# Shared experts of two batches behind the dense experts, the last shared product behind the expert loop, a vector-engine bias, down weights as 128 and 48 rows, and a new order of stages

## The reference

```python
x = x + attention(norm(x))      # q = x Wq + bq, (k, v) = x Wkv + bkv; per token: softmax over 16 heads of q.k, times v
x = x + dense_experts(norm(x))  # 2 experts, 1024 hidden; each token goes to the one with the larger gate
x = x + state_scan(norm(x))     # delta = softplus(...); h = dA * h + dBu along the 512 tokens, 8 states; y = h.C + x * D
x = x + experts64(norm(x))      # 64 experts, 176 hidden, 6 per token, + a shared expert of 352 hidden for all tokens
```

## Time and profile before

| | before |
|---|---|
| median of 3 runs | 772.27 us (769.51 to 773.78) |
| the profiled execution | 767.52 us, of which 765.4 is its span |
| PE busy | 627.5 us, 82% |
| DVE busy | 507.1 us, 66% |
| ACT busy | 198.2 us, 26% |
| POOL busy | 107.1 us, 14% |
| chain that ended last | PE 41%, DVE 33%, DMA 12%, issue 6%, ACT 5% |
| DMA | 114.20 MB, mean 149 GB/s |

### The profile page before, as it was taken

One profiled execution on the slowest core, in us unless ns is written; L12 is line 12 of the kernel. 1 busy time (PEld: TensorE's weight loads), 2 busy tenths in 40 slices (PEclk: granted clock), 3 DMA queues, 4 the chain that ended last, 5 costly groups with the idle time before them and its releaser, 6 DMA issues.

```text
span 765.4 us, 7184 instructions
## 1 busy us (share of the span) xinstructions
PE 627.5 (82%) x2257; PEld 347.0 (45%) x2257; DVE 507.1 (66%) x1096; ACT 198.2 (26%) x387; POOL 107.1 (14%) x119
## 2 busy tenths in 40 slices
PE   4869999889997689999898997573865898888485
PEld 2434555536563446555364554321442544433264
DVE  6773767057993669995588998499957254443355
ACT  1111222145421164331542321512101122212100
POOL 3020220300002000020000020000000355553200
PEclk9999999899999699999798998577977799978889
DMA  9910000429000075010460010998350299997397
GB/s 324 373 49 21 27 22 8 123 85 336 1 34 28 0 265 190 9 40 15 183 237 0 2 62 0 326 307 227 93 169 11 69 309 334 311 292 248 127 405 301
DMA packets 46600, 114.20 MB, mean 149 GB/s; under 512 B 5284, under 2 KB 32037, under 8 KB 46053
## 3 DMA queue, kind: packets, MB, share of 16 engines
q1 hardware_dynamic: 38804, 94.74, 36.5%
q0 software_dynamic: 5456, 16.91, 6.9%
q10 hardware_dynamic: 2304, 2.10, 0.8%
HBM read 84.11 MB, written 29.62 MB: 149 GB/s over the span
## 4 chain that ended last, share of the span: by engine, by line
PE 41%; DVE 33%; DMA 12%; issue 6%; ACT 5%; SPq 2%; POOL 1%; DVEq 0%; POOLq 0%; ACTq 0%
DVE scan_area L1198 8%; PE gate_ps L666 6%; PE up_ps L666 5%; DVE scan_area L1201 4%; DVE scan_area L1194 4%; DMA big<-in_wd 4%; PE turn_ps L638 4%; PE turn_ps L617 3%; DMA bc<-part_rows 3%; PE misc_ps L765 3%; DMA front_area<-in_wd 3%; PE gate_ps L794 3%; PE misc_ps L683 3%; DVE sig L1138 2%; PE turn_ps L639 2%
## 5 line engine op out<-in xcount | busy, mean ns | idle before, releaser
L666 PE MATMUL gate_ps<-big,front_area 128*128 x160 | 86.8, 669 | 1.9 <-ACT front_area L847 1.1
L666 PE MATMUL up_ps<-big,front_area 128*128 x160 | 78.3, 613 | 0.0
L716 PE MATMUL ssm_ps<-scan_area,ident 128*128 128x512 f32 x128 | 64.3, 639 | 15.7 <-DVE scan_area L1201 15.7
L1198 DVE TENSOR_TENSOR_SCAN scan_area<-scan_area 128x1024 f32<-128x1024 f32 x32 | 73.3, 2292 | 5.3 <-ACT scan_area L947 1.8
L683 PE MATMUL misc_ps<-big,front_area 128*128 x320 | 72.5, 380 | 0.9 <-ACT front_area L847 0.9
L1138 DVE SCALAR_TENSOR_TENSOR sig<-sig,gate_ps 128x512 f32<-128x512 f32 (+1 forms) x52 | 35.5, 683 | 55.0 <-ACT sig L883 54.8
L683 PEld LDWEIGHTS misc_ps<-big,front_area 128*128 128x128 f32 x320 | 60.6, 190 | 17.6 <-issue 10.3
L883 ACT ACTIVATE sig<-gate_ps 128x512 f32<-128x512 f32 (+1 forms) x52 | 30.9, 594 | 131.7 <-PE up_ps L666 89.7
L666 PEld LDWEIGHTS up_ps<-big,front_area 128*128 128x128 f32 x160 | 32.6, 204 | 43.2 <-issue 43.2
L947 ACT ACTIVATE scan_area<-scan_area,a_col 128x511 f32<-128x511 f32 x64 | 41.9, 712 | 37.1 <-DVE scan_area L1198 35.7
L617 PE MATMUL turn_ps<-ident,front_area 128*128 128x128 f32 x208 | 33.6, 292 | 21.9 <-DVE front_area L1049 9.7
(11 more groups left out here) (205 smaller groups left out, 931.5 us busy)
## 6 DMA issues: line engine op xcount, KB each, us to landing
bc<-bc_dram SPq DMA_DIRECT2D x4, 4096.0 KB, 13.5
part_rows<-zeros SPq DMA_DIRECT2D x16, 768.0 KB, 16.3
big<-in_wgu SPq DMA_DIRECT2D x15, 704.0 KB
front_area<-in_wgu SPq DMA_DIRECT2D x9, 704.0 KB
big<-part_rows SPq DMA_DIRECT2D x8, 768.0 KB, 10.1
big<-in_wd SPq DMA_DIRECT2D x15, 352.0 KB
scan_area<-in_wgu SPq DMA_DIRECT2D x6, 704.0 KB
front_area<-part_rows SPq DMA_DIRECT2D x5, 768.0 KB, 22.1
```

The costliest lines, as they stand in the source:

```text
L666: mm = pe.matmul(bank[:], xs_t[:, k, j, :], gu0[:, expert_of[b, j], k, g, half * 512:(half + 1) * 512], start=(k == 0), stop=(k == K - 1))
L716: mm = pe.matmul(ssm_ps[:], ident[:], hs[:, g % HS_RING, n, :], start=False, stop=(g % PER_CHUNK == PER_CHUNK - 1 and n == GROUP - 1))
L1198: nc.vector.tensor_tensor_scan(buf.rearrange(flat), d_a[:, g % 2, :, :].rearrange(flat), buf.rearrange(flat), 0.0, ALU.mult, ALU.add).then ...
```

## The change

- **Bias.** `b_qkv` becomes a row spread over all 128 partitions, and DVE adds it to the copied q, k, v of a batch in one operation of 128x1152 elements (`attn_score`). The one-row product on PE goes.
- **Second buffer.** `gate_t` of batch 1 lies in the memory of `mix`, which only the attention and the dense gate use; the others share the old one. In the new `plan` the shared experts of batches 0 and 1 stand behind the last dense down product, around the start of batch 3's scan. `mix` is also memory of the loop's weight ring, so the transfers of pairs 5 to 7 wait for batch 1's `shared_mm` as well.
- **Last shared product.** `shared_out.3` is no stage any more: PE computes it behind the loop into `up_ps`, and DVE adds it there (`last_filled`, `last_added`). In front of the loop PE waits for the last shared silu. `shared.3.1` and `shared.3.2` stand behind `tables.3`.
- **Down weights.** The 176 hidden rows are cut into 128 and 48 instead of 88 and 88. A pair's down weights arrive in two transfers of 512 floats in each partition. The transposes and down products keep their number and their columns.
- **Order.** `plan` is written anew, also in parts that the other edits don't touch: `attn_qkv.2.2` and `.2.3` stand behind `ffn_in.0`, `gates_in.2` in front of `ssm_exp.3`, `shared_out.2.1` behind `gates.3`.

The core of the diff:

```diff
-FC = F1 // 2
+F_ROWS = [P, F1 - P]
...
-        gate_t = sb("gate_t", [P, K, J, P])
+        gate_mem = [sb("gate_t", [P, K * J * P])[:], in_front["mix"]]
+        gate_t = [gate_mem[b == 1].rearrange("p (k j t) -> p k j t", k=K, j=J) for b in range(B)]
...
+        b_qkv = sb("b_qkv", [P, QKV])
...
-            ffn_down.3.4 shared_mm.1.0 ssm_sum.2.5 shared.1.0 shared_mm.1.1 shared_mm.1.2 ssm_sum.2.6 ssm_sum.2.7
-            ssm.2.7 shared.1.1 shared.1.2 ffn_out.3 shared_out.1.0 move_sum.2.1 ssm_out.2 ssm_norm.3 shared_out.1.1
-            ssm_in.3 ssm_proj.3 ssm_exp.3 gates_in.2 ssm_delta.3 gates.2 ssm_a.3.0 ssm_a.3.1 ssm_sum.3.0 ssm.3.0
...
-            ssm_sum.3.5 move_sum.3.1 ssm_sum.3.6 ssm_sum.3.7 rounds.2.2 shared_out.2.0 ssm_out.3 shared_out.2.1
-            gates_in.3 gates.3 shared_mm.3.0 places.3 rounds.3.0 rounds.3.1 shared_mm.3.1 shared.3.0 rounds.3.2
-            shared_mm.3.2 shared.3.1 shared.3.2 tables.3 shared_out.3.0 shared_out.3.1"""
...
+            ssm_a.2.5 ssm_a.2.6 ssm_sum.2.4 ssm.2.5 ffn_down.3.3 ssm.2.6 ffn_h.3.8 ssm.2.7 ffn_h.3.9 ssm_sum.2.5
+            ssm_a.2.7 ffn_down.3.4 rounds.1.2 shared_mm.0.0 move_sum.2.1 shared.0.0 ssm_sum.2.6 ssm_sum.2.7 ssm_out.2
+            ffn_out.3 ssm_norm.3 shared_mm.0.1 shared_mm.0.2 ssm_in.3 ssm_proj.3 gates_in.2 shared.0.1 shared.0.2
+            shared_out.0.0 ssm_exp.3 ssm_delta.3 shared_out.0.1 shared_mm.1.0 shared.1.0 ssm.3.0 ssm_a.3.0 ssm_a.3.1
+            shared.1.1 shared.1.2 shared_mm.1.1 shared_mm.1.2 gates.2 shared_out.1.0 ssm_a.3.2 ssm.3.1 shared_out.1.1
...
+            gates_in.3 gates.3 shared_out.2.1 shared_mm.3.0 places.3 shared_mm.3.1 shared_mm.3.2 shared.3.0
+            rounds.3.0 rounds.3.1 rounds.3.2 tables.3 shared.3.1 shared.3.2"""
...
                     sp.wait_ge(x_after_ffn, B * J)
+                    sp.wait_ge(gu_used, gu_uses_to("shared_mm", 1, 2))
...
-                sp.dma_start(dn1[p % RING], wd1[p, :, :, :]).then_inc(pair_loaded[p % RING], 16)
+                for c, rows in enumerate(F_ROWS):
+                    sp.dma_start(dn1[p % RING][c], wd1[p, c * P:c * P + rows, :]).then_inc(pair_loaded[p % RING], 16)
...
-                pe.matmul(turn_ps[slot][:, 0:QKV], ones[64:65, :], b_qkv, start=False, stop=True
-                          ).then_inc(turn_filled, 1)
+                mm.then_inc(turn_filled, 1)
...
             turn_rows(0)
+            pe.wait_ge(gu_used, shared_used[B - 1])
             run_pairs(pair)
...
+            for h in range(2):
+                shared_down(up_ps[h], h).then_inc(last_filled, 1)
...
+                tt(qkv, qkv, b_qkv[:].unsqueeze(1).broadcast_to([P, J, QKV]), ALU.add).then_inc(attn_steps, 1)
...
+            for h in range(2):
+                dve.wait_ge(last_filled, h + 1)
+                xb = x_res[:, bass.ds((B - 1) * J + 2 * h, 2), :]
+                tt(xb, xb, up_ps[h][:].rearrange("p (j d) -> p j d", j=2), ALU.add).then_inc(last_added, 1)
```

More of the change, by code:

```diff
@@ L164, in pairs_in @@
                 gu1.append(mem[:, at_gu:at_dn].rearrange("p (a f) -> p a f", a=4))
[L165 removed]
+                dn1.append([mem[0:rows, at_dn + c * 2 * D:at_dn + (c + 1) * 2 * D] for c, rows in enumerate(F_ROWS)])
         pairs_in(big, AHEAD_IN_BIG)
@@ L383, in build @@
-            ssm.1.7 ssm_a.1.7 ssm_sum.1.5 shared_mm.0.2 move_sum.1.1 ssm_sum.1.6 ssm_sum.1.7 shared.0.1 shared.0.2
-            ffn_out.2 ffn_in.3 shared_out.0.0 ffn.3.0 ssm_out.1 ssm_norm.2 ffn.3.1 shared_out.0.1 ffn_h.3.0 ffn.3.2
-            ssm_in.2 ffn_h.3.1 ssm_proj.2 gates_in.1 ssm_exp.2 ssm_delta.2 ffn.3.3 ffn_down.3.0 ffn_h.3.2 gates.1
-            ssm.2.0 ssm_a.2.0 ssm_a.2.1 ffn.3.4 ffn_h.3.3 ffn.3.5 ffn_down.3.1 ffn_h.3.4 places.1 rounds.1.0 ssm.2.1
-            ssm_sum.2.0 ssm.2.2 ssm.2.3 ffn.3.6 ssm_a.2.2 ssm_a.2.3 ffn_h.3.5 ffn.3.7 ffn_down.3.2 ssm_sum.2.1
@@ new lines, in build @@
+            ffn_h.2.0 ssm_out.0 gates_in.0 ssm_norm.1 gates.0 ffn.2.2 ssm_in.1 ssm_proj.1 ffn_h.2.1 ssm_exp.1
+            ffn_load.3 places.0 ssm_delta.1 ffn.2.3 ffn_down.2.0 ssm.1.0 ffn_h.2.2 ffn.2.4 ssm.1.1 ssm_a.1.0
+            ssm_a.1.1 ffn_h.2.3 ffn.2.5 ffn_down.2.1 ssm.1.2 ssm_a.1.2 ssm_sum.1.0 ffn_h.2.4 ffn.2.6 ffn_h.2.5
+            ffn.2.7 ssm.1.3 ssm.1.4 ssm_a.1.3 ssm_a.1.4 ffn_down.2.2 ffn_h.2.6 rounds.0.0 rounds.0.1 ssm_sum.1.1
+            ssm_sum.1.2 ffn.2.8 ffn_h.2.7 ffn.2.9 rounds.0.2 ssm_sum.1.3 ssm.1.5 move_sum.1.0 ssm_a.1.5 ssm.1.6
@@ L410, in rings, with gu_uses_to @@
             return Ring(2), Ring(1), Ring(2), Ring(1)
+        def gu_uses_to(*last):
+            done = order[0:order.index(last) + 1]
+            return sum(2 if name == "shared_mm" and s == 2 else 1 for name, _, s in done if name in ("ffn", "shared_mm"))
         def run(eng, stages, skips=()):
```

119 lines of the change are left out of this document (63 added, 56 removed).

## The result

| | before | after |
|---|---|---|
| median | 773.02 us (4 runs, 769.51 to 774.48) | 723.02 us (4 runs, 720.47 to 725.50) |
| ratio | 1 | 0.9359, 95% interval 0.9307 to 0.9411 |
| the profiled execution | 767.52 us, span 765.4 | 720.47 us, span 718.7 |

The change makes the kernel 49.5 us faster by the ratio, 46.7 by the spans of the two traces. Predicted were 734 us and 720 to 754. The direction and the range held; against the traces the sum of the steps, -38.7, was 8 us too small, and the two places where it was most too small are not the ones that I had put rivals on. Ratios and verdicts leave out executions that show a low clock throughout (of the kernel with the last product in front one of 906.02 us, at 0.64).

The account below looks back on a forecast made before the run. PE was taken to limit the attention and dense parts, DVE batch 3's scans, and PE then late down weights the loop. The terms summed to -38.7 us, from a median of 772.27 to 734 us, range 720 to 754.

Parts of the forecast that it names:

- (a): Attention part and batch 3: bias leaves PE for a DVE addition; -7.5 us, and -2 for batch 3's pairs.
- (b): Dense part: batch 0's shared experts move out, PE loses 15.8 us and DVE follows; -14 us, bounds -4 and -15.8.
- the rival's -4: Dense part: DVE, not PE, holds it, so moving the shared experts gives only -4 us; total 744, chance 0.20.
- (c): Batch 3's turn from dense to scan: norm starts at 462.7 against 466.82, -4.1 us; gathers become what is late.
- the sign that I gave for (c): Batch 3's turn from dense to scan: DVE's dense output of batch 3 waits for its gather.
- (d): Scan stage of batch 3 takes in displaced shared-expert work: +6.4 us, bounds +3 and +12, at a higher clock.
- a sign of being wrong: Scan stage of batch 3: PE waits appearing between its scans would show the prediction wrong.
- (e): Before the loop: last shared product and silus leave the path, shared_out.2.1 enters it; -7.5 us, -5 to -9.5.
- (f): Expert loop: down weights as 128 and 48 rows use sixteen engines instead of eleven; -10 us, bounds 0 and -11.8.
- The cap: Expert loop: PE is late next at 3.1 us a pair, limiting the split's gain to 11.8 us.
- The rival of the half-rate piece: Expert loop: the 48-row piece moves at half rate, so the split gives only -4 us; total 740, chance 0.15.
- (g): Behind the loop: last shared product, 5.4 us on PE, fits its idle wait for stored rows; 0, up to 5.4.

Follow-up runs that it names:

- the kernel with the last product in front: Changed kernel with both halves of shared_out.3 run ahead of the loop again, nothing of them behind it: 725.61 us, ratio 0.9431 to before.
- the old order: Changed kernel with the plan's order of before, shared_out.3 dropped from it, everything else as changed: 733.54 us, ratio 0.9556 to before.
- the one with batch 1's turn as before: Changed kernel with only ffn_out.1, ffn_in.2 and ffn.2.0 put back behind two scan sums and move_sum.0.1: 727.84 us, ratio 0.9485 to before.
- 96 and 80 rows: Changed kernel with down weights cut into 96 and 80 rows instead of 128 and 48: 735.01 us, ratio 0.9570 to before.

## Why the prediction was right, point by point

**(a) Bias**, -9.5 with batch 3's pairs: -9.8 at the first dense product of batch 1, and undone alone +10.9 by the spans. Right in size. The first dense product came at 64.5 (63.5 foretold), and the addition takes 1.34 us (1.38 foretold). Its split into 7.5 and 2 fits the old order, which has 63.4 and 72.2 in the first two columns against 71.0 and 75.8 before; in the new one, where the last projections of batch 2 stand behind the first dense product, undoing the bias costs 3.2 and 6.3.

**Missing: the turn of batch 1.** The sum had nothing for it; its column lost 5.7 us, up to 3.6 of it by the two scan sums that went to the next column, and the turn alone is worth 7.3 in all. I had read the new order only where shared experts move, and passed over three names that change places there. This is the largest error of the sum.

**(b) Batch 0's shared experts**, -14: batch 2's column lost 10.3, of which the order gives 9.9. But the column now begins ahead of the two scan sums of batch 1, 3.6 us of PE. With these in front of it, as they are in the kernel before and in the one with batch 1's turn as before, it is 115.6 and 102.7: -12.9, near my -14 and far from the rival's -4. PE's work in the column fell by 11.7 us (102.7 to 91.0) and DVE's by 6.2, so DVE did follow, as I had it (15.8 us of products left PE's share of the column, and the 3.6 of the sums came in). The experts' own share in this is not measured alone.

**(c) Turn from dense to scan of batch 3**, -4.1: the column lost 9.2, the order alone 8.9. The kernel after, to be read against the earlier trace rows:

```profile
415.95 3.62 PE L692 MATMUL misc_ps<-big,front_area 128*128 x16
...
426.03 0.95 POOL L584 DMA_INDIRECT front_area<-ysorted_dram,slot_idx  x1 [0.30 <-issue]
...
430.14 1.67 DVE L1174 SCALAR_TENSOR_TENSOR x_res<-front_area,slot_w,x_res 128x256 f32<-128x256 f32 x4 [0.16 <-DVE x_res L1229]
431.85 1.41 DVE L1038 BATCH_NORM_STATS2 ln_st<-x_res 128x6 f32<-128x256 f32 x4
```

From the end of the last down product to the norm 20.5 us became 12.3. The mis-sized term is the end of that product: I put one more scan sum ahead of it, 3.4 us, and it ended no later against the first dense product of batch 3 than before (92.6 us behind it, 93.5 before). (b) and (c) together were -18.1 and are -19.5. The gathers and DVE are late at nearly the same time; the row names DVE's own addition, not the gather, so that the sign that I gave for (c) did not appear.

**(d) Last scans take the work in**, +6.4: +7.8, and -9.4 when the order is undone. Right in sign, and in size for this trace; that it is so near is partly luck, since three other kernels with this very order have 102.8 or 102.9 in the column, +12.2, at the lower clock. DVE's waits for PE's down products are 11.6: 7.43 us where 9.64 of idle time were before, 2.84 where I had counted about 1, and 1.35 (1.82 before). The second is a wait for PE between the scans of batch 3, which I had named as a sign of being wrong. The granted clock rose from 0.79 to 0.87, as foretold.

**(e) Before the loop**, -7.5: 47.1 became 38.6, -8.4. To the indices it is -2.1 (-4.8 + 3.3 by my working), from there to the loop -6.4 (-6.0). The wait for `shared_out.2.1` on DVE, which takes most of the gain at the indices back, is there:

```profile
547.64 0.69 DVE L1309 TENSOR_TENSOR x_res<-x_res,misc_ps 128x512 f32<-128x512 f32 x1 [3.44 <-PE misc_ps L777]
...
567.70 0.66 PE L797 MATMUL turn_ps<-ident,bc 128*128 128x128 f32 x2 [4.23 <-DMA bc<-table,att_s]
568.91 1.44 PE L806 MATMUL gate_ps<-big,bc 128*64 128x352 f32 x4 [0.55 <-ACT bc L998]
```

PE now waits for the gather, 4.23 us, as foretold; undone alone this part costs 5.5 to 6.4.

**(f) Split**, -10: the loop lost 11.3. Right in the difference and wrong in the mechanism. I took the gain to be that of sixteen engines for eleven, at a fixed rate per engine. The share of 0.70 that I read it from is the tail of a stretch, and it moves gate and up weights as well (84 of their 5632-byte rows and 81 down rows of 4096 bytes), so it gives no price for down weights alone. In the loop of the kernel before the DMA share is 1.01 from 620 to 640, at 333 GB/s; the kernel after has 1.03 and 365. And 96 and 80 rows, with the share of all engines, keep a loop of 110.7 us. What the split gives is more bytes at the same share, and why is open. The cap was not what I thought either: in the kernel before PE's pace is 2.79 with gaps, in the kernel after 3.08 without a gap, since the 48-row product costs 0.29 us a pair. That both give about 3.1 is chance. Undone in the changed kernel the split costs 20.6 us of loop, as PE then drains the ring at 2.79 and waits at 5.6 us a pair. The rival of the half-rate piece asked for a gain of 4 us and falls by the size. Why the same 88-row transfers take 118.0 us here and 108.7 in the kernel before is not settled; in the last third they move 248 GB/s here (640 to 660) and 290 there (670 to 690).

**(g) Last product behind the loop**, 0: +0.3. PE works on it for 5.46 us and then still waits 2.89 for stored rows, against 8.69 in the earlier trace rows:

```profile
671.84 5.46 PE L777 MATMUL up_ps<-w_shd,hsh_t 128*128 128x256 f32 x24
680.19 4.34 PE L851 MATMUL gate_ps<-big,ident 128*128 128x256 f32 x12 [2.89 <-DMA big<-part_rows]
```

The sum of the measured terms: -9.8 - 5.7 - 10.3 - 9.2 + 7.8 - 8.4 - 11.3 + 0.3 = -46.6 against -38.7. Undone one at a time, the bias, the order, the split and the last product cost 12, 15, 23 and 5.5 us by the ratios, 56 in all against 49.5 for the whole. The terms don't simply add: the split's 23 stands against the 11.3 that its column lost.
